# Interaction tower on one core: scratch writes between gathers, the split of the one-hot work, and who moves the pair values

## What is computed

```python
e = jnp.stack([tbl_0[ids[:, 0]], ..., tbl_26[ids[:, 26]]], axis=1)   # 512 x 27 x 128, fp32
interactions = jnp.einsum('bnd,bmd->bnm', e, e)
i, j = jnp.triu_indices(27, k=1)
z = interactions[:, i, j]                                            # 512 x 351
h = jnp.concatenate([z, dense_ctx], axis=1)                          # 512 x 367
h = jnp.maximum(h @ W_top1 + b_top1, 0.0)                            # 512 outputs
h = jnp.maximum(h @ W_top2 + b_top2, 0.0)                            # 256 outputs
y = h @ W_top3                                                       # 512 x 1
```

## Time and profile before

| | |
|---|---|
| median of 3 runs | 138.52 us (138.08 to 139.58) |
| profiled execution | 138.44 us |
| its span, first to last instruction | 136.5 us |
| TensorE clock granted, mean over the span | 0.912 |
| busy: PE, DVE, ACT, POOL | 116.4, 77.6, 65.2, 76.3 us |

### The profile page before, as it was taken

One profiled execution on the slowest core, in us unless ns is written; L12 is line 12 of the kernel. 1 busy time (PEld: TensorE's weight loads), 2 busy tenths in 40 slices (PEclk: granted clock), 3 DMA queues, 4 the chain that ended last, 5 costly groups with the idle time before them and its releaser, 6 DMA issues.

```text
span 136.5 us, 2480 instructions
## 1 busy us (share of the span) xinstructions
PE 116.4 (85%) x1016; PEld 93.8 (69%) x1016; DVE 77.6 (57%) x67; ACT 65.2 (48%) x106; POOL 76.3 (56%) x92
## 2 busy tenths in 40 slices
PE   5679989999698987989895697757899989999894
PEld 5546767777486775867674465535699969899791
DVE  2499999999999999999602020200435011531221
ACT  4099998999949696596030203002422111151021
POOL 2187888788788787888889989987000000001300
PEclk9999999999999999999999755555579999999999
DMA  3987787888675869941121112551144410003300
GB/s 58 325 340 175 245 255 243 275 199 264 225 237 168 243 143 362 352 94 38 38 56 44 38 38 58 179 102 53 45 126 111 106 27 0 0 5 130 74 0 1
DMA packets 15103, 18.67 MB, mean 137 GB/s; under 512 B 8767, under 2 KB 10905, under 8 KB 14964
## 3 DMA queue, kind: packets, MB, share of 16 engines
q1 hardware_dynamic: 12932, 14.20, 34.5%
q0 software_dynamic: 2016, 4.06, 10.6%
q10 hardware_dynamic: 144, 0.26, 1.1%
HBM read 16.74 MB, written 1.77 MB: 136 GB/s over the span
## 4 chain that ended last, share of the span: by engine, by line
PE 39%; DVE 36%; issue 16%; DMA 6%; ACT 1%; SPq 0%; ACTq 0%; DVEq 0%
DVE hot L432 24%; PE psG L332 18%; DVE parts L437 11%; PE psH L347 5%; PE psH L377 4%; DMA pick_ids<-in_picked_ids 3%; PE psT L295 3%; PE psG L315 3%; PE psG L359 3%; DMA pair_blocks<-gram 2%; PE psH L390 2%; DMA zT<-pair_blocks 1%; ACT gram L526 1%; DVE ET L422 1%; SPq L162 0%
## 5 line engine op out<-in xcount | busy, mean ns | idle before, releaser
L273 POOL DMA_INDIRECT rows<-in_tbl,ids_sb x60 | 65.4, 1090 | 19.7 <-issue 15.1
L315 PE MATMUL psG<-hot,parts 128*128 128x512 f32 x216 | 55.4, 403 | 7.4 <-DVE hot L432 2.9
L315 PEld LDWEIGHTS psG<-hot,parts 128*128 128x128 f32 x216 | 38.6, 188 | 20.8 <-DVE hot L432 6.5
L432 DVE TENSOR_TENSOR hot<-pick_ids,psH 128x1536 fp32r<-128x1536 int32 (+1 forms) x24 | 47.4, 2014 | 3.3 <-DMA pick_ids<-in_picked_ids 3.3
L332 PE MATMUL psG<-ET 128*52 128x54 f32 x512 | 25.1, 248 | 8.1 <-issue 7.0
L332 PEld LDWEIGHTS psG<-ET 128*52 128x52 f32 x512 | 20.6, 154 | 13.2 <-issue 11.8
L445 DVE COPY gram<-psG 128x432 f32<-128x432 f32 x8 | 7.2, 903 | 30.4 <-remote 19.8
L526 ACT COPY gram<-psG 128x432 f32<-128x432 f32 x8 | 7.2, 898 | 28.4 <-remote 19.8
L170 POOL DMA_DIRECT2D zT<-pair_blocks x2 | 1.7, 869 | 30.5 <-DMA pair_blocks<-gram 30.5
L437 DVE TENSOR_TENSOR parts<-table,parts 128x1024 fp32r<-128x1024 f32 (+1 forms) x12 | 16.2, 1352 | 0.0
L514 ACT ACTIVATE hot<-pick_ids,row_no 128x512 fp32r<-128x512 int32 x24 | 16.2, 727 | 0.0
(11 more groups left out here) (27 smaller groups left out, 40.5 us busy)
## 6 DMA issues: line engine op xcount, KB each, us to landing
table<-in_tbl SPq DMA_DIRECT2D x6, 640.0 KB
table<-in_tbl SPq DMA_DIRECT2D x6, 512.0 KB, 6.5
pick_ids<-in_picked_ids SPq DMA_DIRECT2D x11, 256.0 KB, 3.9
pair_blocks<-gram SPq DMA_DIRECT2D x8, 216.0 KB, 2.4
w_sb<-in_w SPq DMA_DIRECT2D x1, 1024.0 KB
rows<-in_tbl,ids_sb POOLq DMA_INDIRECT x60
w_sb<-in_w SPq DMA_DIRECT2D x1, 512.0 KB
zT<-pair_blocks SPq DMA_DIRECT2D x7, 63.0 KB
```

The lines of the kernel that those rows point to most:

```text
L273: pool.indirect_dma_start(out=rows[:, n % RING, x, :], out_offset=None, in_=gathered_tables[f], in_offset=bass.IndirectOffsetOnAxis(ap=ids ...
L315: last = pe.matmul(psP[:, k % 2, :], parts[:, k % 2, x, c, :], hot[:, k % 2, c, :], start=x == 0 and c == 0, stop=x == 1 and c == CH[k] - 1)
L432: dve.tensor_tensor(hot[:, k % 2, first:end, :], pick_ids[:, k % TABLES, :].unsqueeze(1).to_broadcast(shape), numbers.unsqueeze(2).to_broa ...
```

## The change

- `PAUSE` goes from 320 columns to 4, and the scratch write stands behind every gather from the first, not only behind the last 22. Each gather still waits for the write before it.
- For picks with 10 chunks ACT makes three one-hot chunks in place of two, and DVE seven in place of eight; with 8 chunks it stays two and six. ACT's second step is one instruction over all its chunks, behind all of the first steps.
- The second half of each tile's write to DRAM moves from SP to ACT, as do the reads of chunks 2 and 3 of tile 0 and of chunk 1 of tile 3 (which POOL issued before). They are steps of the list.
- Layer 1 of tile 0 goes chunk by chunk in the banks psG, as that of tile 3, and waits until the products of tiles 0 to 2 are copied out of them; its layers 2 and 3 use psG too. `layer3(0)` moves behind `layer1(1)`. The wait for y_ready of tile 0 moves from `layer1(1)` to `layer3(1)`.

```diff
-    BY_ACT = [2] * FP
+    BY_ACT = [2 if chunks == min(CH) else 3 for chunks in CH]
...
-    PAUSE = 320
-    FIRST_PAUSED = 10
+    PAUSE = 4
...
+    BY_CHUNK = (0, T - 1)
+    L1_SIGNALS = [0, N1, N1 + 2, N1 + 4]
+    SP_READS = [(0, 1), (0, 1, 2, 3), (0, 1, 2, 3), (0, 2)]
+    ACT_READS = [(2, 3), (), (), (1,)]
...
-            return psG[:, n // 2, n % 2, 0:P] if t == T - 1 else psH[:, n // 2, n % 2, :]
+            return psG[:, n // 2, n % 2, 0:P] if t in BY_CHUNK else psH[:, n // 2, n % 2, :]
...
         def h2_psum(t, n):
+            if t == 0:
+                return psG[:, 0, 0, P * (n + 1):P * (n + 2)]
...
         def y_psum(t):
+            if t == 0:
+                return psG[0:1, 1, 0, P:2 * P]
...
-        steps = units(0) + quads(9, 10) + units(1) + quads(10, 12) + units(2) + quads(12, 13)
-        steps += mlp(0) + quads(13, 14) + [("layer3", 0)] + mlp(1) + quads(14, 16) + [("layer3", 1)] + units(3)
-        steps += mlp(2) + [("chunk", 0), ("layer3", T - 2), ("chunk", 1), ("chunk", 2),
+        steps = units(0) + [("write", 0)] + quads(9, 10) + units(1) + [("write", 1)] + quads(10, 12) + [("read", 0)]
+        steps += units(2) + [("write", 2)] + quads(12, 13) + mlp(0) + quads(13, 14)
+        steps += [("layer1", 1), ("layer3", 0), ("layer2", 1), ("layer2_end", 1)] + quads(14, 16) + [("layer3", 1)]
+        steps += units(3) + [("write", 3)]
+        steps += mlp(2) + [("read", T - 1), ("chunk", 0), ("layer3", T - 2), ("chunk", 1), ("chunk", 2),
...
-                    sp.wait_ge(last_hot_ready, sum(BY_ACT[:k - TABLES + 1]))
+                    sp.wait_ge(last_hot_ready, k - TABLES + 1)
...
-                for x in range(S):
-                    write_blocks(sp, t, x)
+                write_blocks(sp, t, 0)
...
-                for c in range(NC) if t < T - 1 else (0, 2):
+                for c in SP_READS[t]:
...
-                    if n >= FIRST_PAUSED:
-                        if pauses:
-                            pool.wait_ge(paused, pauses)
-                        pool.memset(pause[:, :], 0.0).then_inc(paused, 1)
-                        pauses += 1
+                    if pauses:
+                        pool.wait_ge(paused, pauses)
+                    pool.memset(pause[:, :], 0.0).then_inc(paused, 1)
+                    pauses += 1
...
-            read_pairs(pool, T - 1, 1)
...
                             else:
-                                pe.wait_ge(last_hot_ready, sum(BY_ACT[:k]) + c - own + 1)
+                                pe.wait_ge(last_hot_ready, k + 1)
...
-                if t == 0:
-                    pe.wait_ge(w1_in, 16)
-                    pe.wait_ge(dense_in, 16)
-                else:
+                if t > 1:
...
                     for c in range(NC):
-                        last = pe.matmul(psH[:, n // 2, n % 2, :], w1_sb[0:ROWS[c], c, P * n:P * (n + 1)],
+                        last = pe.matmul(h1_psum(t, n), w1_sb[0:ROWS[c], c, P * n:P * (n + 1)],
...
-            def last_layer1(c):
+            def layer1_chunk(t, c):
                 if c == 0:
-                    pe.wait_ge(gram_dve, U * T)
-                    pe.wait_ge(gram_act, U * T)
-                pe.wait_ge(chunk_in[T - 1][c], 16 * len(CHUNKS[c]))
+                    products = U * (T if t == T - 1 else T - 1)
+                    pe.wait_ge(gram_dve, products)
+                    pe.wait_ge(gram_act, products)
+                if c == 0 and t == 0:
+                    pe.wait_ge(w1_in, 16)
+                    pe.wait_ge(dense_in, 16)
+                pe.wait_ge(chunk_in[t][c], 16 * len(CHUNKS[c]))
                 for n in ORDER:
-                    last = pe.matmul(psG[:, n // 2, n % 2, 0:P], w1_sb[0:ROWS[c], c, P * n:P * (n + 1)],
-                                     zT[0:ROWS[c], T - 1, c, :], start=c == 0, stop=c == NC - 1)
+                    last = pe.matmul(h1_psum(t, n), w1_sb[0:ROWS[c], c, P * n:P * (n + 1)],
+                                     zT[0:ROWS[c], t, c, :], start=c == 0, stop=c == NC - 1)
...
-                if t < T - 1:
+                if t not in BY_CHUNK:
...
-                if t < T - 1:
...
+                elif t < T - 1:
+                    pe.wait_ge(y_ready, t)
...
+                elif step == "layer1" and x in BY_CHUNK:
+                    for c in range(NC):
+                        layer1_chunk(x, c)
...
                 elif step == "chunk":
-                    last_layer1(x)
+                    layer1_chunk(T - 1, x)
...
                 for n in range(2):
-                    dve.wait_ge(l1_done, 2 * t + 1 + (2 * n if t == T - 1 else 0))
+                    dve.wait_ge(l1_done, L1_SIGNALS[t] + 1 + (2 * n if t in BY_CHUNK else 0))
...
-                for x, c in enumerate(chunks):
-                    act.wait_ge(distance_ready, sum(BY_ACT[:k]) + x + 1)
-                    act.activation(hot[:, k % 2, c, :], hot[:, k % 2, c, :], ACT.Relu, bias=1.0, scale=-1.0
-                                   ).then_inc(last_hot_ready, 1)
+                act.wait_ge(distance_ready, sum(BY_ACT[:k + 1]))
+                last = hot[:, k % 2, chunks[0]:CH[k], :]
+                act.activation(last, last, ACT.Relu, bias=1.0, scale=-1.0).then_inc(last_hot_ready, 1)
...
+            def write_half(t):
+                act.wait_ge(gram_dve, U * (t + 1))
+                act.wait_ge(gram_act, U * (t + 1))
+                write_blocks(act, t, 1)
...
+            def read_half(t):
+                act.wait_ge(blocks_out[t], 16 * S)
+                for c in ACT_READS[t]:
+                    read_pairs(act, t, c)
...
                 for n in range(2, 4):
-                    act.wait_ge(l1_done, 2 * t + 2 + (2 * (n - 2) if t == T - 1 else 0))
+                    act.wait_ge(l1_done, L1_SIGNALS[t] + 2 + (2 * (n - 2) if t in BY_CHUNK else 0))
...
+                elif step == "write":
+                    write_half(x)
+                elif step == "read":
+                    read_half(x)
```

## The result

The changed kernel takes 155.36 us (155.06 to 155.48, 4 runs) against 138.30 for the kernel before on the same chip: the ratio is 1.124, with a 95% interval of 1.119 to 1.128. The forecast was 131.4, with a range of 129.0 to 136.5. The profiled execution took 155.37 us, with a span of 153.5.

A forecast was written before the change was run, and what follows sets the result against it. Bounds: DVE's pace in the picks to 70 us, then gathers that slow PE's products, then PE's own work. 138.44 - 6.0 (products end earlier) - 1.1 (behind them) = 131.3, median 0.08 above: 131.4; range 129.0 to 136.5.

The forecast's parts named there:

- the fourth gather of a pick not locked out: In the picks, the fourth gather fits before the next subtraction by 0.12 us; rival that it is locked out: 136.0, chance 0.14.
- The sum behind the products: Stages after the products of tiles 0 and 1: 0.8 - 0.5 + 0.4 + 0.4 = 1.1 us gained.
- The 0.4 of that term: Tile 3's two writes issued side by side land 0.6 us earlier, ending PE's 0.4 us wait for chunk 0.
- part 1: One-hot work: DVE's second comparison, shorter by 0.53 us in each of six picks, saves 3.2 us on the path.
- Part 3: Products of tiles 0 and 1 under the gathers: they end at 90.1 us in place of 96.14, gaining 6.0.
- nothing passes beside the short pauses: Rival for the products of tiles 0 and 1: 200 records remain at 86.5 us, end 94.7; total 136.0, chance 0.08.
- the rate by time: Products of tiles 0 and 1: records keep passing at 7.96 a us while gathers run, 139 in 17.5 us.
- in mid-gather: Sign against "nothing passes beside the short pauses": some bursts of product records begin in the middle of a gather.
- The rule of the Trainium skill: TensorE never waits on anyone, so the thin product rate is PE's own; as a rival 136.3 us, chance 0.07.
- all on the clock: Rival: clock stays low in tile 2's products and layers of tiles 0 and 1; return at 110 gives 140.2; chance 0.05.
- the end at 88.2: Products of tiles 0 and 1 end at 88.2 us if records pass by the gather, 11.9 each; total 129.4.
- ACT half exposed: Upper end of own range, 133.0 us: half of ACT's possible 2.6 us of extra pick work is not hidden.

The follow-up runs named there:

- a_relief_2: Changed kernel with scratch writes of 820 columns behind every fourth of the first 38 gathers, 320 behind the last 22: 141.6 us beside 139.7 for the kernel before.
- after_again: The changed kernel run once more, nothing altered: 155.4 us beside 139.7 for the kernel before (1.113).
- b_short_late: Kernel before with scratch writes of 4 columns in place of 320, still only behind the last 22 gathers: 143.66 us (1.035).
- g_sp_loads_2: Kernel before with its 60 gathers replaced by plain 128-row loads issued by SP, without the look-up: 124.0 us beside 138.9 (0.895).
- a_tail_only_2: Changed kernel with the scratch writes and one-hot split of the kernel before: 138.4 us beside 138.9 (0.996).
- g_pool_long: Kernel before with gathers replaced by plain SP loads, without look-up, and POOL doing 60 scratch writes of 1440 columns: 121.1 us beside 139.4 (0.869).
- w_640: Changed kernel with the old one-hot split and old write places, but 640 columns in place of 320: 127.5 us beside 139.4 for the kernel before (0.915).
- g_sp_loads: Kernel before with its 60 gathers replaced by plain SP loads, without look-up: 124.9 us on a chip where the kernel before took 121.0.

## Why the prediction was wrong

**The sizes held.** Comparison 2.28 us, picks 5.27 apart, ACT's merged step 1.49, write 0.12 (0.10 expected), gathers 1.26 apart (1.22), the fourth gather of a pick not locked out (36.94 and 42.20 are four apart). The sum behind the products was 1.0 for 1.1, though not in its parts. Tile 2's products ran at full clock (0.8), `layer1` of tile 0 waited 0.5, and `layer1(1)` didn't wait for y, as expected. But ACT's write of tile 1 held back its copy of quad 11, and the two writes side by side took as long as one behind the other: 3.02 us from issue to landing here,

```profile
139.01 3.02 DMA pair_blocks<-gram
142.04 2.27 DMA zT<-pair_blocks
```

where rows 8 have 3.07 from 122.21 to 125.28. PE waited 0.7 for chunk 0 and not 0. The 0.4 of that term was not there.

**The step that failed is in part 1: "DVE sets the pace, so this is on the path."** It put the first product at 67.3 us; it came at 107.06. The step treats the 0.8 us in each pick in which the subtraction holds a gather as a cost to POOL alone. These 0.8 us are free time for PE too. a_relief_2 keeps the short picks, gives such time back in another way, and has no stall. The shorter pick leaves the four gathers and takes 0.53 of the 0.8 us away. Then the signals fall behind: in after_again ACT waits for "remote" 1.06 us at 42.18, 2.19 at 45.03 and 24.45 at 74.59. DVE and ACT stop, no subtraction holds a gather any more, and from then on little gets through until POOL waits for its ring (from 75 us) or the gathers are done. That last step, the hold growing on itself, is my reading of these rows; no run tests it by itself.

**Part 3 had the right resource and the wrong reach.** The rival "nothing passes beside the short pauses" was nearly true in both halves: with four columns 1.5 records a us pass, with 320 5.6 to 9.4. So the term "the rate by time", 7.96 a us beside short pauses, failed too: b_short_late, the short pauses without the rest, took 4.8 us more than the kernel before. I gave the rival 0.08 and 136.0 us. Its price was wrong in two ways. I applied it to the products only, and I let PE run as soon as the gathers end, where in b_short_late the hold went on 3.3 us longer. The row that should have warned me was the wait for "remote": if PE's signals come late too, every stage with gathers is exposed, the picks as well. The bursts "in mid-gather", which I took as a sign against it, are there, but they come in both kernels and say nothing of the rate.

**The rule of the Trainium skill** (SBUF — State Buffer, "SBUF: two separate sides"), that TensorE waits on no one, doesn't cover what these runs show: with POOL's gathers away, 323 records of the products went through in place of 151 (g_sp_loads_2 and a_tail_only_2, 72 to 88 us). Whether a port has to do with it was not tried; g_pool_long shows that POOL's writes to SBUF do not.

**The chance of a slower kernel was 0.05**, all on the clock. The clock was not it: the page has it back at its upper level from 100 us on, once PE had dense work, and tile 2's products ran at that level.

Two of the sums of the range are off by tenths, which changes nothing: the end at 88.2 gives 129.5 and not 129.4, and ACT half exposed (1.3 us) gives 132.7 and not 133.0.

What in a gather holds PE up, and whether it is PE's fetch of work or the path of its signals that suffers, is open. So is what sets the chips apart.

## What to carry to other kernels

Where one engine crawls only while another does a certain work, look for what spaces that work out, and count these gaps as a resource before shortening them; idle or held time of an engine off the critical path can be what another engine lives on. Look also at who waits for signals of the crawling engine ("remote" or "issue" waits that end together on several engines), as that tells how far the hold reaches. And try the gap's length first, in both directions: 320 more columns of a useless write were worth 12 us here (139.4 to 127.5; w_640 has the rest of the change too, which a_tail_only_2 shows to be worth nothing that can be told), and four in place of 320 behind the last gathers cost 5 (138.8 to 143.7).

## What the runs showed of the hardware

- While POOL issues indirect gathers 1.25 us apart, PE gets 1.5 to 2.9 pair-product records a us through; 5.6 to 9.4 with 0.55 us between gathers, 17 with 0.82 (w_640), and 38 with none beside it. What waits for its signals started up to 30 us late (75.66, the changed kernel). The kernel before took 138 to 140 us on each of four chips.
- With gathers 1.25 us apart the hold outlasted the last of them by 3.3 us (b_short_late, 90.33 to 93.61).
- On a fifth chip the same kernel took 121.0 us, with no hold. The cause of the difference is not known, and a comparison of kernels with gathers across chips says nothing. With plain loads in place of the gathers it took 124.9 us there (g_sp_loads) and 124.0 on a chip with the hold (g_sp_loads_2).
- A DVE instruction with two inputs in SBUF holds a gather that starts under it (1.75 in place of 0.95 us), but not a scratch write (0.39 at 66.17, rows 4).
